# Adding gathered expert rows inside the DMA, and the score mask on GpSimd in 28 of 64 steps

## The reference

```python
xn = layernorm(x)
s = attention(xn)           # 32 heads of 8, keys i-8 <= j < i+8
g = silu(moe(xn))
return x + s * g

# attention: scores q k * scale, multiplied by a fixed weight (8 - |i-j|/2)/8
# inside the band and set to -inf outside it, softmax, times v, projection, bias
# moe: each row goes to the one expert (of 8) with the largest logit
for e in range(8):
    xe = where(expert_idx == e, x * sigmoid(max_logit), 0)
    out += where(expert_idx == e, (silu(xe @ gate_w[e]) * (xe @ up_w[e])) @ down_w[e], 0)
shared = (silu(x @ shared_gate_w) * (x @ shared_up_w)) @ shared_down_w
return out + shared
```

## Time and profile before

| | |
|---|---|
| median of 3 runs | 634.32 us (633.57 to 634.75) |
| profiled execution | 633.25 us, its span 631.4 us |
| TensorE busy | 557.1 us (88%) |
| VectorE busy | 403.7 us (64%) |
| ScalarE busy | 307.9 us (49%) |
| GpSimd busy | 187.0 us (30%) |
| mean granted TensorE clock | 0.978 |

### The profile page before, as it was taken

The page is one execution under the profiler, slowest core; times in us unless marked ns, Lnnn a source line. Parts: engine busy times, 40 slices in busy tenths (PEclk is TensorE's granted clock), DMA queues, the critical chain, the costliest instruction groups (busy, mean ns, idle before and its releaser), DMA issues. The chain is left out here.

```text
span 631.4 us, 10599 instructions
## 1 busy us (share of the span) xinstructions
PE 557.1 (88%) x3358; PEld 479.0 (76%) x3358; DVE 403.7 (64%) x853; ACT 307.9 (49%) x762; POOL 187.0 (30%) x160
## 2 busy tenths in 40 slices
PE   1979999979889999999999999999886877769865
PEld 1757898758768999888999888898675655657754
DVE  6766556885756446456446456446688888886873
ACT  1473654458673644533634533645454533636331
POOL 6001011148861111000111000114655545532230
PEclk9989999979999999999999999999989899999997
DMA  8525441113327576576577566443133333331110
GB/s 292 180 70 174 151 141 55 49 49 99 113 92 216 163 223 202 167 203 199 143 218 208 168 203 190 126 129 115 50 110 110 108 99 101 117 102 26 35 42 17
DMA packets 107371, 82.89 MB, mean 131 GB/s; under 512 B 42293, under 2 KB 104757, under 8 KB 107317
## 3 DMA queue, kind: packets, MB, share of 16 engines
q1 hardware_dynamic: 98628, 68.72, 36.9%
q0 software_dynamic: 3072, 8.39, 4.2%
q10 hardware_dynamic: 5616, 5.11, 2.3%
HBM read 59.12 MB, written 23.07 MB: 130 GB/s over the span
## 5 line engine op out<-in xcount | busy, mean ns | idle before, releaser
L427 POOL TENSOR_TENSOR Sx<-Sx,mx 128x752 f32<-128x752 f32 x64 | 93.7, 1465 | 407.1 <-DVE mx L729 406.5
L945 PE MATMUL psV<-VB,PTs 128*128 128x132 f32 x1024 | 133.1, 282 | 30.2 <-ACT Or L470 29.7
L945 PEld LDWEIGHTS psV<-VB,PTs 128*128 128x128 f32 x1024 | 127.1, 193 | 36.1 <-issue 34.9
L470 ACT ACTIVATE Or<-psV 32x128 f32<-32x128 f32 x256 | 68.5, 268 | 150.5 <-DVE rs L759 146.2
L920 PE MATMUL psS<-kBD,qBD 128*128 128x188 f32 x512 | 104.0, 327 | 0.0
L920 PEld LDWEIGHTS psS<-kBD,qBD 128*128 128x128 f32 x512 | 86.9, 193 | 10.4 <-issue 2.2
L751 DVE STREAM_TRANSPOSE PTs<-Sx 128x512 f32<-128x512 f32 x128 | 82.9, 685 | 1.0 <-ACT Sx L500 1.0
L995 PE MATMUL psM<-xT,EB 128*128 128x128 f32 x624 | 76.4, 276 | 0.0
L995 PEld LDWEIGHTS psM<-xT,EB 128*128 128x128 f32 x624 | 73.8, 192 | 2.1 <-ACT qBD L489 1.3
L722 DVE TENSOR_TENSOR Sx<-psS,cst 128x752 f32<-128x752 f32 x64 | 59.6, 932 | 24.5 <-PE psS L920 24.5
L736 DVE SCALAR_TENSOR_TENSOR ea<-et,psM 128x256 f32<-128x256 f32 x39 | 16.4, 421 | 76.3 <-PE psM L995 47.2
(11 more groups left out here) (107 smaller groups left out, 689.3 us busy)
## 6 DMA issues: line engine op xcount, KB each, us to landing
EB<-in_L_ffn_gate_w SPq DMA_DIRECT2D x39, 256.0 KB, 2.9
EB<-in_L_ffn_up_w SPq DMA_DIRECT2D x39, 256.0 KB, 3.6
EB<-in_L_ffn_down_w SPq DMA_DIRECT2D x39, 256.0 KB, 3.1
VB<-v_dram SPq DMA_DIRECT2D x256, 32.0 KB
stage<-xs_dram SPq DMA_DIRECT2D x39, 128.0 KB, 2.2
ys_dram<-yb ACTq DMA_DIRECT2D x39, 128.0 KB, 3.1
xs_dram<-blank SPq DMA_DIRECT2D x9, 512.0 KB, 3.8
v_dram<-vS SPq DMA_DIRECT2D x8, 512.0 KB, 2.9
```

The lines of the kernel that those rows point to most:

```text
L427: nc.gpsimd.tensor_tensor(s, s, mx[n % 3][:, :].unsqueeze(2).broadcast_to([P, 2 * G, KW]), ALU.subtract).then_inc(a_sub, 1)
L470: return nc.scalar.activation(dst, src, ACT.Copy)
L945: last = mm(psV[:, j, at:at + HS * VW], PTs[n % 2][:, k, j, i, :], VB[n % 2][:, i, k, :, VW * j:VW * j + VW], start=k == 0, stop=k == 1)
```

## The change

Three edits that go together.

1. `masked_late(n)` holds in steps 0 to 7 and in the 20 steps with pairs of experts (18 to 37). There TensorE leaves out the two mask matmuls, GpSimd adds the mask (new `banded`, in place on Sx, after `weigh` and before `largest`), and VectorE does `largest` after `flipped(n - 1)` and not right after `weigh`. The mask in float32, repeated to the layout of the scores, comes with the constants: `cst` grows by 12 x 47 = 564 columns.
2. The gathers no longer write to Y. They add into the shared rows on the way (`compute_op=ALU.add`); `combine` is gone. `gather(c)` waits for the shared rows of its chunk (`f_sh`) and is issued in the step ahead of ScalarE's `silu(c)`, behind that step's subtraction.
3. ScalarE's `silu(c)` waits for the gather's DMAs (`d_y`) and for the buffer Y to be read (`d_w`).

```diff
-C_STAY = C_HEAD + HS
+C_BAND = C_HEAD + HS
+C_STAY = C_BAND + 12 * KW
...
+def masked_late(n):
+    return n < BATCH or E0 <= n < E0 + NP
...
+            def banded(n):
+                pool.wait_ge(a_mul, n + 1)
+                s = Sx[n % 3][:, :, :].rearrange("p (m r) k -> p m r k", r=HS)[:, :, :, 0:KW]
+                kind = 2 * KC * mask_kind(n)
+                nc.gpsimd.tensor_tensor(s, s, band[:, kind:kind + 2 * KC, :].unsqueeze(2).broadcast_to([P, 2 * KC, HS, KW]),
+                                        ALU.add).then_inc(a_add, 1)
...
             def gather(c):
-                b = c % 3
                 if c == 0:
                     for k in range(3):
                         pool.wait_ge(b_st[k], 16 * len(range(k, NX, 3)))
-                if c >= 3:
-                    pool.wait_ge(d_w, c - 2)
+                pool.wait_ge(f_sh, c + 1)
                 for k in range(CT):
                     t = c * CT + k
-                    pool.indirect_dma_start(Y[b][:, k * C:(k + 1) * C], None, ys_dram,
-                                            bass.IndirectOffsetOnAxis(ap=slot[:, t:t + 1], axis=0)).then_inc(d_y[b], 16)
-
-            def combine(c):
-                b = c % 3
-                z = shared_rows(c * CT).rearrange("p t c -> p (t c)")
-                pool.wait_ge(d_y[b], 16 * CT * (c // 3 + 1))
-                pool.wait_ge(f_sh, c + 1)
-                nc.gpsimd.tensor_tensor(z, Y[b], z, ALU.add).then_inc(d_z, 1)
+                    pool.indirect_dma_start(shared_rows(c * CT)[:, k, :], None, ys_dram,
+                                            bass.IndirectOffsetOnAxis(ap=slot[:, t:t + 1], axis=0),
+                                            compute_op=ALU.add).then_inc(d_y[c % 3], 16)
 
             for n in range(LAST + 1):
-                for c in silu_at(n):
-                    combine(c)
                 if n < U:
+                    if masked_late(n):
+                        banded(n)
                     subtract(n)
...
-                if n == C_STEP:
-                    for c in range(3):
-                        gather(c)
-                for c in silu_at(n - 1):
-                    if c + 3 < NC:
-                        gather(c + 3)
+                for c in silu_at(n + 1):
+                    gather(c)
...
             def silu(c):
-                act.wait_ge(d_z, c + 1)
+                act.wait_ge(d_y[c % 3], 16 * CT * (c // 3 + 1))
+                if c >= 3:
+                    act.wait_ge(d_w, c - 2)
...
             def largest(n):
-                dve.wait_ge(a_mul, n + 1)
+                if masked_late(n):
+                    dve.wait_ge(a_add, len([k for k in range(n + 1) if masked_late(k)]))
+                else:
+                    dve.wait_ge(a_mul, n + 1)
...
                     weigh(n)
-                    largest(n)
+                    if not masked_late(n):
+                        largest(n)
...
                     flipped(n - 1)
+                if n < U and masked_late(n):
+                    largest(n)
...
                 for j in range(KC):
-                    mm(psS[:, j, 0:BW], identb[:, :], maskb[:, kind:kind + 2, :, :].rearrange("p i r k -> p (i r k)"),
-                       start=True, stop=False)
+                    if not late:
+                        mm(psS[:, j, 0:BW], identb[:, :], maskb[:, kind:kind + 2, :, :].rearrange("p i r k -> p (i r k)"),
+                           start=True, stop=False)
```

More of the change, by code:

```diff
@@ L91, in constants @@
     c[:, C_MASK:] = np.concatenate([np.where(k, 0.0, NEG) for k in kinds], 1)
+    c[:, C_BAND:C_STAY] = np.tile(c[:, C_MASK:].reshape(P, 3, 1, 2 * KW), (1, 1, KC, 1)).reshape(P, 12 * KW)
     return c
@@ L216, in build @@
         ident = cst[:, C_ID:C_ID + P]
+        band = cst[:, C_BAND:C_BAND + 12 * KW].rearrange("p (m k) -> p m k", k=KW)
         mw = cst[:, C_M:C_M + KW]
@@ L240, in build @@
         m_full = [sem(f"m_full{i}") for i in range(MB)]
-        a_qk, a_S, a_mul, a_max, a_sub, a_exp, a_PT, a_V, a_PV, a_O, a_rec, a_nrm, a_OT, a_s = (
-            sem("a_" + n) for n in ("qk", "S", "mul", "max", "sub", "exp", "PT", "V", "PV", "O", "rec", "nrm", "OT", "s"))
+        a_qk, a_S, a_mul, a_add, a_max, a_sub, a_exp, a_PT, a_V, a_PV, a_O, a_rec, a_nrm, a_OT, a_s = (
+            sem("a_" + n) for n in ("qk", "S", "mul", "add", "max", "sub", "exp", "PT", "V", "PV", "O", "rec", "nrm", "OT", "s"))
         x_v, x_vd = ([sem(f"x_{n}{i}") for i in range(2)] for n in ("v", "vd"))
@@ L248, in build @@
         d_y, d_x, d_st = ([sem(f"d_{n}{i}") for i in range(3)] for n in ("y", "x", "st"))
-        d_z, d_t, d_w, d_g, d_o = (sem("d_" + n) for n in ("z", "t", "w", "g", "o"))
+        d_t, d_w, d_g, d_o = (sem("d_" + n) for n in ("t", "w", "g", "o"))
         x_tiles = x.rearrange("(t p) c -> p t c", p=P)
@@ L907, in scores @@
                 h, u = divmod(n, UH)
-                if n == 0:
+                late = masked_late(n)
+                if n == BATCH:
                     pe.wait_ge(s_cast, 2)
@@ L920, in scores @@
                         last = mm(psS[:, j, i * HS * KW:(i + 1) * HS * KW], qBD[h % 2][:, j, k, :, :].rearrange("p s q -> p (s q)"),
-                                  kBD[h % 2][:, j, :, k * QB:k * QB + KW], start=False, stop=i == 1)
+                                  kBD[h % 2][:, j, :, k * QB:k * QB + KW], start=late, stop=late or i == 1)
                 last.then_inc(a_S, 1)
```

## The result

The changed kernel takes 630.57 us in the median of 6 runs (629.18 to 631.63), the kernel before 633.89 (6 runs): a ratio of 0.9946 with a 95% interval of 0.9929 to 0.9964. It is faster, by 3.3 us, where 14.2 were forecast. The profiled execution has a span of 627.9 us.

A forecast was written before the change was run, and what follows sets the result against it. Bound: TensorE in pair steps, the VectorE-ScalarE ring with GpSimd in its way in the gather stretch. 8.7 + 13.5 + 2.5 - 3 x (1.6 + d) - (1.2 + 2d) = 18.7 - 5d, 14.2 us: 620.1 us, range 611 to 631.

The forecast's parts named there:

- The mask: Pair steps and steps 0 to 7: mask matmuls taken off TensorE gain 8.7 us, start included, bounds 6.3 to 9.7.
- The cover ahead of `largest`: VectorE's transposes and, to step 6, `normalise` hide GpSimd's mask add; a 0.3 us stall in step 7 and pair steps.
- The combine: Gather stretch: without GpSimd's combines VectorE gets 13.5 us back, plus 2.5 us of ScalarE's wait for the first combine.
- three q steps: Steps 44, 48 and 52, where ScalarE also copies q and half of k: psV copies 1.6 + d late each.
- d: What the addition costs over a plain gather, per chunk: taken as 0.9 us, between below 0 and 3.5.
- The last two chunks: Chunks 14 and 15, gathered only once their shared rows are copied: tanh late, cost 1.2 + 2d.
- (b): Rival: GpSimd writes more per row, d = 1.9, or 2.6 with landing doubled; 625 to 628.6 us; chance 0.18.
- the other steps lose nothing: Gather steps without copies of q and k: most have 2.4 us of room, so no loss below d = 2.6.
- (a): Rival: the addition is free, d = 0, 615.6 us, or 610.8 if the q steps' 4.8 is hidden; chance 0.13.
- (e): Rival: GpSimd's gather issues hold VectorE as the combine did; gain only 0.7 us, no change; chance 0.03.
- (c): Rival: the mask moves its cost, late subtractions make ScalarE wait, 8.7 us not gained: 628.8 us; chance 0.06.
- (d): Rival: slower; added rows land late, past d = 2.6 all gather steps wait; 635.8 us at d = 3.5; chance 0.11.

The follow-up runs named there:

- the first experiment: Only the mask's part of the change, with the gathers, combines and ScalarE's waits of the kernel before: 625.05 us, ratio 0.9868 to the kernel before.

## Why the prediction was wrong

**Right.** The mask: 8.7 us forecast, 8.9 measured alone, 1.26 and 1.27 us per cycle of the pair steps. That the total fits so well is partly luck: in the trace of the mask's part step 8 is reached 3.2 us sooner (2.4 forecast with the start), and steps 8 to 37 give 5.4 (6.3 forecast). The cover ahead of `largest`: a stall of 0.56 us in step 7 and in each pair step, 11.8 us in 21 steps, where 0.3 was forecast, since the addition takes 1.66 us there and not 1.45; it costs nothing in the pair steps from 20 on, though step 18 is 0.55 us longer than before (7.48 for 6.93). The combine: 16.0 us forecast, 17.0 measured without it, and L768 (now L775) takes 0.28 or 0.29 us in all steps. The place of the first loss: three q steps, 1.6 us each with d = 0 (1.8 measured). The last two chunks: 1.2 + 2d is 5.3 with the measured d of 2.05; steps 60 to 62 take 24.45 us for 19.03 with no combine, 5.4. Here too two errors meet: with d = 0 they lose 2.3 us and not 1.2, and the addition adds 3.2 and not 4.1.

**The size of d.** It was put at 0.9 us, as the nearest row, between bounds of 0 and 3.5; it measures 1.7 to 2.05. Most of it is not in the landing, where the second read from which the 0.9 came would show, but in GpSimd's issue, twice 0.6 us, which stood in rival (b). With 5d in the sum this is 5 x 1.15 = 5.8 us, and the sum would have read 8.4. The prediction named an issue past 1.5 us as a sign of being wrong, and it came: 1.62 in the mean.

**The step that failed.** "Chunks 14 and 15 can be gathered only when their shared rows are copied." So can chunks 12 and 13: the shared expert of the seventh sequence is copied in steps 52 and 53, the very steps in which their gathers now stand. The kernel before could gather these early, since only its combine needed the shared rows. With more lead for all chunks before them, steps 53 and 54 still take 9.96 and 9.12 us, for 7.04 and 7.57 with no combine: 4.5 us (4.7 in the changed kernel). The same step of the prediction said that below d = 2.6 "the other steps lose nothing", for steps of 7.1 to 7.6 us. Step 41 lasts 5.87, and step 42 loses 1.1 us (9.80 for 8.66 with more lead).

The whole account, by step lengths against the kernel without the combine: 11.1 us are lost in the three q steps, 4.7 in steps 53 and 54, 5.4 in steps 60 to 62 and 1.1 in step 42, together 22.4 where 10.5 were forecast (7.5 and 3.0). With the 17.0 and 8.9 that come back the gain is 3.5; measured are 3.3.

**The rivals.** Of (a) to (e), (b) is the nearest: a dearer issue and a d of 1.9 are what was found, and its 625 to 628.6 lacks chunks 12 and 13 and step 42. (a) falls by d, (c) and (e) by the first experiment and by `result` at 0.68 us, and the d of 2.6 from which (d) starts was not reached. That GpSimd writes more for each row was not seen as such. What the queue shows is 6144 packets for 3072, all of the increase in 32 gathers, so 144 for 48 each, at the same 8.39 MB. In the Trainium skill, *Collectives: The Full Stack*, section "The bandwidth ceiling: the fold count and why AG ≠ RS ≠ AR", an addition emits two read descriptors per chunk where a copy emits one. The trace agrees in that there are more packets, but one read added to a read and a write would make three of two, not three of one, and the runs do not show which of them are reads.

## What to carry to other kernels

Work taken off an engine pays only if the consumer's new wait is as loose as the old one: when a copy and an add become one adding transfer, it inherits the latest of both inputs, so list for each instance when the destination is ready, not only for those at the end. A transfer's cost that no trace shows should be multiplied by how often it stands on the path before one settles on a value; here a factor of 5 stood ahead of it (7 by the runs), and with one more step of lead and the last chunks later ScalarE waited 2.0 us in all. When GpSimd work sits between two VectorE instructions, put other VectorE work between them where VectorE has no idle time: here that was worth 14 us in steps 0 to 7, 2.4 in steps 18 and 19, and nothing in steps 20 to 35.

## What the runs showed of the hardware

An adding indirect DMA costs GpSimd 1.55 us of issue for 128 rows of 1 KB where a plain one costs 0.96. Both take longer when they start while VectorE is inside an instruction with two SBUF inputs: the adding issue 1.95 us at 437.04, with 0.53 us of L807 left, and 1.72 at 485.33, with 0.29 left; the plain one, in the run without the addition, 1.32 at 524.75, with 0.48 left. An issue within which L807 begins (511.72) keeps its 1.55, and the VectorE instructions keep their 0.65 and 0.68 us. The adding gather lands 2.30 us after the issue's end in the median instead of 1.83. The GpSimd addition of the mask, whose second operand is rows of 47 values used for four heads each, takes 1.66 us in the pair steps and 1.75 beside `normalise` in most of steps 0 to 6, where the subtraction of one value per row of 47 takes 1.45; whether the operand's shape or the operation is the reason was not tried.
